# The down product taken two tiles behind in a two-block transformer kernel

## What is computed

```python
h = _layernorm(x) * (1 + ca) + sa
x = x + ga * _L0_attn_ref(h, ...)          # delta-rule scan, state 64, then RMS norm and Wo
h = _layernorm(x) * (1 + cb) + sb
x = x + gb * _L0_ffn_ref(h, ...)           # silu(gate) * up, RMS norm, ternary weights, width 2048
h = _layernorm(x) * (1 + ca) + sa
x = x + ga * _L1_attn_ref(h, ...)          # token shift, K, V, R products, exponential scan, Wo
h = _layernorm(x) * (1 + cb) + sb
x = x + gb * _L1_ffn_ref(h, ...)           # silu(gate) * up, integer codes as weights, width 1408
```

## Time and profile before

| | |
|---|---|
| median of 3 executions | 1342.05 us (1340.87 to 1342.58) |
| the profiled execution | 1341.83 us, of which the trace spans 1340.1 us |
| mean granted TensorE clock | 0.87 of full speed |
| TensorE matmul busy | 1154.2 us (86%) |
| VectorE busy | 887.4 us (66%) |
| ScalarE busy | 539.0 us (40%) |
| GpSimd busy | 167.7 us (13%) |
| all 16 DMA engines | 56 GB/s over the span |

### The profile page before, as it was taken

How to read it: one execution, slowest core, us unless ns; L and a number is a source line. 1 busy time by engine, 2 the same in 40 slices (tenths; PEclk the granted TensorE clock), 3 DMA queues, 4 the chain that set the end, 5 groups by cost and what they waited for, 6 DMA issues and landing times. The chain is left out here.

```text
span 1340.1 us, 13543 instructions
## 1 busy us (share of the span) xinstructions
PE 1154.2 (86%) x4553; PEld 609.5 (45%) x4599; DVE 887.4 (66%) x1647; ACT 539.0 (40%) x1147; POOL 167.7 (13%) x151
## 2 busy tenths in 40 slices
PE   6656899778757889998889989899898999989997
PEld 5425765756533334443444434444443444434443
DVE  3466545677654576788765879857969377873554
ACT  2343545445414433553414535326433254341321
POOL 3000000000002222221202212112210100010100
PEclk9665855566657999999989999999999999999999
DMA  8400000352143530000100102111211001100000
GB/s 257 157 32 16 1 1 32 126 173 95 64 155 108 185 114 0 12 28 24 55 8 1 32 16 63 48 32 39 76 40 40 0 16 63 47 1 32 0 32 32
DMA packets 38821, 75.57 MB, mean 56 GB/s; under 512 B 3702, under 2 KB 7286, under 8 KB 38624
## 3 DMA queue, kind: packets, MB, share of 16 engines
q1 hardware_dynamic: 37760, 72.50, 16.4%
q0 software_dynamic: 992, 2.21, 0.6%
HBM read 66.16 MB, written 8.54 MB: 56 GB/s over the span
## 5 line engine op out<-in xcount | busy, mean ns | idle before, releaser
L1400 PE MATMUL g_g<-h,wt 128*128 128x512 f16 x1728 | 399.4, 382 | 4.2 <-DVE hid L1576 2.1
L1400 PEld LDWEIGHTS g_g<-h,wt 128*128 128x128 bf16 (+1 forms) x1728 | 168.8, 98 | 227.6 <-issue 32.9
L1412 PE MATMUL g_d<-wt,parts 128*128 128x512 bf16 (+1 forms) x829 | 200.0, 381 | 14.2 <-DVE parts L1581 7.6
L1805 ACT ACTIVATE parts<-hid 128x512 f16<-128x512 f32 x108 | 68.2, 631 | 299.8 <-DVE hid L1576 294.4
L1348 PE MATMUL g_o<-xmix,w_kvr 128*128 128x512 f32 x384 | 179.8, 612 | 9.0 <-DVE tmp L1494 6.6
L1569 DVE SCALAR_TENSOR_TENSOR hid<-th,g_g 128x512 f32<-128x512 f32 x108 | 73.5, 681 | 159.4 <-ACT th L1798 159.3
L1412 PEld LDWEIGHTS g_d<-wt,parts 128*128 128x128 f16 x864 | 82.7, 98 | 125.8 <-issue 16.2
L1348 PEld LDWEIGHTS g_o<-xmix,w_kvr 128*128 128x128 f32 x384 | 74.8, 196 | 90.7 <-issue 70.8
L1906 POOL TENSOR_TENSOR acc<-acc,sqh 128x512 f32<-128x512 f32 x52 | 75.1, 1444 | 308.3 <-ACT sqh L1811 308.3
L1581 DVE TENSOR_TENSOR parts<-hid,parts 128x512 f16<-128x512 f32 x108 | 83.0, 768 | 31.2 <-ACT parts L1805 31.1
L646 PEld LDWEIGHTS sc<-gatedw,LT 128*128 128x128 f32 x320 | 65.9, 281 | 34.9 <-DVE gatedw L997 21.6
(11 more groups left out here) (277 smaller groups left out, 1665.0 us busy)
## 6 DMA issues: line engine op xcount, KB each, us to landing
wmod<-in_wmod SPq DMA_DIRECT2D x12, 1024.0 KB, 6.6
w_raw<-in_wt SPq DMA_DIRECT2D x24, 512.0 KB, 4.0
w_kvr<-in_w SPq DMA_DIRECT2D x48, 256.0 KB, 2.7
xmix<-in_codes SPq DMA_DIRECT2D x16, 528.0 KB, 4.2
codes_f<-xmix SPq DMA_DIRECT2D x16, 264.0 KB, 2.1
gates<-in_x SPq DMA_DIRECT2D x4, 1024.0 KB, 5.6
x<-in_x SPq DMA_DIRECT2D x4, 1024.0 KB, 10.8
xmix<-in_wo SPq DMA_DIRECT2D x4, 1024.0 KB, 5.2
```

The source lines that it names most:

```text
L1400: mm = nc.tensor.matmul(pg[i][:], wide[:, k, o:o + P], h16[f % 2][:, s, k], start=(s == 0 and k == 0), stop=(s == 1 and k == KD - 1))
L1412: mm = nc.tensor.matmul(pd[j][:], parts16[:, t % 3, s, j * P:(j + 1) * P], wd[:, m, :], start=(m == 0 and s == 0), stop=(done and s == 1))
L1805: nc.scalar.activation(parts16[:, t % 3, 0], hid[:, t % 2], ACT.Copy).then_inc(hi_ready, 1)
```

## The change

Four places move, and nothing is added or taken out.

```diff
-    ATT = [54 + 54 * i for i in range(NG)]
+    ATT = [57 + 54 * i for i in range(NG)]
...
-            if t:
-                product(t - 1)
+            if t >= 2:
+                product(t - 2)
             side(3 * t + 2)
+        product(TILES - 2)
         product(TILES - 1)
...
-            start = f and t == min(first_tile(f) + 1, TILES)
+            start = t == TILES or (f and t == first_tile(f) + 2)
...
-                if t == first_tile(NG + i + 1) + 2:
+                if t == first_tile(NG + i + 1) + 3:
                     store_x(i)
```

## The result

The changed kernel takes 1347.50 us in the median of 7 executions (1343.55 to 1347.97), the kernel before beside it 1340.87 us (1339.04 to 1342.58). The ratio is 1.0044, 95% interval 1.0030 to 1.0058: **slower by 0.44%**. Its profiled execution is the fastest of the seven: 1343.55 us, span 1341.8 us, mean granted clock 0.87, as before. Measured again later, the ratio was 1.0024 (1.0012 to 1.0036). The two intervals overlap narrowly; both lie above 1.

A forecast was written before the change was run, and what follows sets the result against it. Early tiles were taken as bound by a VectorE and ScalarE loop, 6.66 us a turn against TensorE's 5.18. Terms of both signs summed to +3.0 us on the 1342.05 us median, giving 1345.0, range 1336 to 1352.

The forecast's parts named there:

- Product waits: Tiles 1 to 10: TensorE's 7.6 us of waits for low parts move to other instructions, nothing gained, 0.
- Ends: First and last tiles: one product more is left at the end, the last no longer waits, +1.1 us.
- Tiles 42 to 44: Attention of group 3: TensorE stops only for the last mixed product, 34.9 us instead of 41.8, -6.9 us.
- Tiles 45 to 48: Transposes of instance 3: ScalarE's slacks stand before the pair freeing a bank, VectorE is late, TensorE stops, +4.6 us.
- Tiles 66 to 70 and 60 to 63: Instance 5, output products no longer share a place with transposes, -3.0 us; instance 4, the same pairs meet again, -0.3 us.
- Tiles 82 to 84: Instance 6: a mixed product behind the transposes waits 21.8 to 27.8 for a bank ScalarE frees, +5.5 us.
- Boundaries: Tile 34, VectorE starts residual rows later, +2.0 us; tile 50, sums no longer give VectorE cover, +1.7 us.
- what keeps its distance: Residual rows, a group's first product and second mixer all move one tile, so waits among them stay; costed at nothing.
- A: Rival, 8%: the early gap is slack after all and the loop gives way, 7.7 us gained, 1337 us.
- B: Rival, 18%: VectorE is on time at tiles 82 to 84 and 45 to 48, both terms about +1, 1337 us.
- C: Rival, 18%: stalls only move; gains and losses cancel within a boundary's reach, 1342 us.
- D: Rival, 8%: the long stop at tile 84 brings more half clock and the next boundary starts late, 1352 us.

The follow-up runs named there:

- lag only: The kernel before with the product two tiles later, a group's last two both in the next group's first tile; mixer, residual rows unmoved: 1346.95 us, ratio 1.0035.
- its variant with the later preparation: The changed kernel with the preparation rows of instance 6 one tile later (250 in place of 247): 1342.67 us, ratio 1.0017 against the kernel before.
- the changed kernel with the mixer at 60: The changed kernel with the second mixer one tile later still (60 in place of 57): 1333.92 us, ratio 0.9959 against the kernel before.
- slide only: The kernel before with the second mixer alone one tile later, product and residual rows as before: 1337.66 us, ratio 0.9968.

## Why the prediction was right

Forecast: 3.0 us of loss, 1345.0 us. Measured: 3.4 and 3.6 us in `groups` in two traces, +0.44% and +0.24% in the medians. The side and the size came out, the first median 2.5 us over. The sum is nearer than its terms, which were off by up to 1.7 us with both signs; that they cancel to 0.4 us is partly luck. By the steps:

- *Product waits, 0.* Right over tiles 0 to 15, and shown by lag only: the loop of VectorE and ScalarE sets the pace. Tiles 1 to 9 take 53.3 us in the changed kernel against 54.3, tiles 0 to 15 are 0.3 us longer. The Trainium skill, Perfetto Trace Analysis, "Optimization Strategy", reads a repeated gap as a possible lack of buffers; here the tile more of slack paid 1.0 us in tiles 1 to 9, which was gone by tile 16. Not foreseen was that the waits, once off the products, merge: 1.36 and 0.59 us into one of 3.02 us, with half clock behind it in two traces of the changed kernel.
- *Ends, +1.1.* Measured +1.0 behind tile 93. The last products run in one row.
- *Tiles 42 to 44, -6.9.* Predicted 34.9 us, measured 35.5, which is -6.3.
- *Tiles 45 to 48, +4.6.* Measured 47.1 us; less the mixed product that moved in (3.4) that is 3.9 over 39.8. The stops of the prediction add up to 6.6 us against 1.6, so its term should have read +5.0; its "rounding against me" went the other way.
- *Tiles 66 to 70 and 60 to 63, -3.0 and -0.3.* The 67.4 us of the earlier trace rows are those of tiles 65 to 70. They took 56.3 us with the change, with two side products fewer (6.9), so -4.2. Tiles 60 to 63 gave +0.6, in the second trace +2.2. The whole stretch 55 to 72 gave -3.4 against -3.3.
- *Tiles 82 to 84, +5.5.* Predicted 41.0 us, measured 41.5, with the wait (6.0 predicted, 6.34 measured) and the half clock where they were put. It makes up the loss of the stretch 73 to 92, +5.7.
  The Trainium skill's rule on banks in rotation (Perfetto Trace Analysis, "Matmuls"), taken alone, would have made this term and the +4.6 nothing; both waits are in the trace, at banks that do rotate.
- *Tiles 27 to 31, -1.7.* Measured 59.5 us against 61.2: -1.7 (-1.1 in the second trace).
- *Boundaries, +2.0 and +1.7.* The second gave +2.4. The first was wrong in size: tile 33 before took 15.2 us, tile 34 after 15.5. The gap was filled by something that I had costed at nothing ("what keeps its distance"): tiles 18 to 20, the first mixer's start behind the residual rows, went from 21.3 to 22.5 us.

The first rival, A, is out by lag only. B is out by the rows of tile 84. C is not cleanly out. Gains and losses did not cancel within a boundary's reach, and both measurements lie above 1; but the waits of TensorE add up to 63 us before and after, and the second ratio, 0.24%, is hardly over the 0.2% that the prediction gave to C. D's long stop and half clock were there, but no late boundary behind them: 15.3 us at the next one against 15.4.

What the prediction did not see is the larger thing. It summed the slide to about nothing, -1.8 without the boundaries, and read the boundaries against the kernel before only. Taken apart, the change is a gain of 6.4 us in the trace (4.3 by the ratio) from the mixer's slide and a loss of about 10 (7.5 to 10 by the ratios) from the product's lag and the later residual rows that go with it. Why the second half loses so much is in part argued. The late residual rows take the slide's room away again: with the lag, but the residual rows where they were, tiles 33 to 35 take 32.5 us against 36.2 and tiles 18 to 20 take 21.3 against 22.5. But no run moves the residual rows alone, since a group's last product moves with them. The weakest step is "the waits among them stay" at cost nothing. As a statement on the change it is nearly true (+1.2 us at tiles 18 to 20); the missed question was whether those waits had to be there.

## What to carry to other kernels

A wait at the consumer is not the place to relax when the rows show that the producers never wait for the consumer: here the wait only moved to the next instructions. When one engine carries several bursts of side work (here residual rows, statistics, reciprocals), try other distances between the bursts, and more than one; here two tiles brought four times as much as one (1.28% against 0.32%), and the slack that had been aimed at brought nothing. Take a change apart into its halves on the chip even where the sum was predicted well, since the halves here were a gain of 4 to 6 us and a loss of 7.5 to 10.

## What the runs showed of the hardware

The same order with the same stop was followed by either clock. The eight transposes behind a stop of 3.0 us (L1316, tile 10) in the changed kernel's timeline,

```profile
479.25 1.94 PE L1316 MATMUL g_o<-ident,hf 128*64 128x128 f32 x8 [3.02 <-DVE hf L1488]
```

and in its variant with the later preparation, which has the same order up to there:

```profile
480.66 1.06 PE L1316 MATMUL g_o<-ident,hf 128*64 128x128 f32 x8 [3.02 <-DVE hf L1488]
```

In the first the clock was granted at 0.50 (1.2 GHz) for 6.8 us and tile 11 took 9.5 us, in the second 7.5. The second trace of the changed kernel is like the first (9.6 us), that of the changed kernel with the mixer at 60 like the second (7.5). By the end of tile 15 the two traces shown differed by 0.3 us: the first had no half clock at 517 us, the second did. So a stretch of half clock that one trace shows at a place is no price of that place by itself. Single traces of one order differ by some 2 to 3 us: tiles 16 to 36 took 198.5, 198.8 and 200.9 us in three traces of the changed kernel's order, and 193.1, 196.2 and 196.3 in three of slide only's. In the last three the granted clock was at half for 3.4, 10.2 and 10.2 us in tiles 27 and 28.
